# Two graph layers on one core: the first 24 index gathers read x in place of the projected source table

## The reference, cut to what matters

```python
def _L0_gnn_ref(h, edge_index, edge_feat, W1, b1, W2, b2, W3, b3, W4, b4):
    msg_input = concatenate([h[src], h[dst], edge_feat], axis=-1)
    messages = silu(msg_input @ W1 + b1) @ W2 + b2
    agg = segment_sum(messages, dst, num_segments=6250)
    h_new = silu(concatenate([h, agg], -1) @ W3 + b3) @ W4 + b4
    return h_new + h
def _L1_gnn_ref(h, edge_index, eps, W1, b1, W2, b2, gamma, beta):
    z = (1.0 + eps) * h + segment_sum(h[src], dst, num_segments=6250)
    r = relu(z @ W1 + b1) @ W2 + b2 + h
    return relu(layernorm(r) * gamma + beta)
x = layernorm(x + _L0_gnn_ref(x, ...))
x = layernorm(x + _L1_gnn_ref(x, ...))
```

## Time and profile before

| | us |
|---|---|
| three runs | 1515.1, 1518.32, 1519.86 |
| median | 1518.32 |
| the profiled execution, its own time | 1517.0 |
| its span | 1514.8 |
| first gather from `src_term` starts | 39.46 |
| last gather from `src_term` starts | 1028.6 |

### The profile page before, as it was taken

The page is one execution under the profiler, slowest core; times in us unless marked ns, Lnnn a source line. Parts: engine busy times, 40 slices in busy tenths (PEclk is TensorE's granted clock), DMA queues, the critical chain, the costliest instruction groups (busy, mean ns, idle before and its releaser), DMA issues.

```text
span 1514.8 us, 31192 instructions
## 1 busy us (share of the span) xinstructions
PE 1273.0 (84%) x8093; PEld 1046.3 (69%) x8093; DVE 1011.0 (67%) x2306; ACT 641.7 (42%) x1257; POOL 1103.0 (73%) x1164
## 2 busy tenths in 40 slices
PE   6577777777787889888888898975999999999993
PEld 6355556665565667676766776754899999998882
DVE  5578886577764566666666565653666778888866
ACT  3735455455554555556555555652111111111111
POOL 1777777777777777777777777776777777777771
PEclk9889999999998999999999999997999999999995
DMA  5423333333335444455445544432887778778731
GB/s 196 119 81 95 87 90 95 93 95 89 92 94 100 129 135 126 125 135 133 126 126 135 131 129 124 132 78 84 260 255 232 220 224 244 229 221 239 218 93 47
DMA packets 189124, 214.15 MB, mean 141 GB/s; under 512 B 60426, under 2 KB 149517, under 8 KB 189011
## 3 DMA queue, kind: packets, MB, share of 16 engines
q1 hardware_dynamic: 138399, 131.62, 28.4%
q0 software_dynamic: 36352, 74.52, 20.7%
q10 hardware_dynamic: 14260, 6.68, 1.5%
HBM read 202.74 MB, written 9.85 MB: 140 GB/s over the span
## 4 chain that ended last, share of the span: by engine, by line
POOL 47%; PE 29%; issue 16%; DMA 4%; DVE 3%; SPq 1%; ACT 0%; DVEq 0%; ACTq 0%; POOLq 0%
POOL gath L869 47%; PE bank L1404 10%; PE bank L1380 8%; PE bank L1332 4%; DMA gath<-src_term,src_col 2%; PE bank L1210 1%; PE bank L1220 1%; PE bank L1206 1%; PE bank L1366 1%; DMA dst_rows<-in_dst 1%; PE bank L1411 1%; PE bank L1353 1%; PE bank L1426 1%; SPq L655 0%; DVE st L1982 0%
## 5 line engine op out<-in xcount | busy, mean ns | idle before, releaser
L869 POOL DMA_INDIRECT gath<-src_term,src_col x784 | 751.4, 958 | 244.2 <-issue 236.0
L869 POOL DMA_INDIRECT gath<-layer_input,src_col x336 | 327.8, 975 | 105.9 <-issue 100.3
L1210 PE MATMUL bank<-gath,ident 128*128 128x512 f32 x392 | 224.2, 655 | 170.0 <-DMA gath<-src_term,src_col 169.7
L1206 PEld LDWEIGHTS bank<-terms_r,terms_l 128*128 128x128 f32 x1568 | 202.4, 195 | 52.6 <-issue 52.4
L1885 DVE TENSOR_SCALAR_CACHE_REDUCE terms_l<-dst_bc,node_col 64x512 f32<-64x512 int32 x196 | 221.2, 1129 | 15.7 <-issue 9.8
L1896 DVE TENSOR_TENSOR S<-S,bank 128x128 f32 x98 | 28.1, 287 | 292.0 <-PE bank L1222 176.0
L1220 PEld LDWEIGHTS bank<-oh,msg 128*128 128x128 f32 x1568 | 201.2, 204 | 29.1 <-issue 28.4
L1206 PE MATMUL bank<-terms_r,terms_l 128*128 128x128 f32 x1568 | 211.2, 279 | 3.3 <-ACT msg L1014 2.5
L1220 PE MATMUL bank<-oh,msg 128*128 128x128 f32 x1568 | 204.2, 287 | 0.0
L1210 PEld LDWEIGHTS bank<-gath,ident 128*128 128x128 f32 x392 | 61.2, 197 | 190.8 <-DMA gath<-src_term,src_col 190.7
L1404 PE MATMUL bank<-S 128*128 128x288 f32 x672 | 170.0, 406 | 0.9 <-DVE S L1955 0.9
(11 more groups left out here) (208 smaller groups left out, 1703.2 us busy)
## 6 DMA issues: line engine op xcount, KB each, us to landing
dst_bc<-in_dst SPq DMA_DIRECT2D x195, 128.0 KB
xT<-sorted_src SPq DMA_DIRECT2D x42, 512.0 KB
xs<-layer_input SPq DMA_DIRECT2D x136, 128.0 KB
gath<-src_term,src_col POOLq DMA_INDIRECT x784
terms_l<-layer_input SPq DMA_DIRECT2D x88, 128.0 KB
terms_r<-layer_input SPq DMA_DIRECT2D x88, 128.0 KB
msg<-layer_input SPq DMA_DIRECT2D x80, 128.0 KB
ef_s<-in_edge_attr SPq DMA_DIRECT2D x97, 64.0 KB
```

The costliest lines, as they stand in the source:

```text
L869: g.indirect_dma_start(out=gath[:, slot, j * D:(j + 1) * D], out_offset=None, in_=table[0:rows, :], in_offset=bass.IndirectOffsetOnAxis(ap ...
L1206: mm(bank[h][:, j * D:(j + 1) * D], terms_l[:, u, h, j, :], terms_r[:, u, h, j, :], start=j == 0, stop=False)
L1210: mm(bank[h][:, :], ident[:, :], gath[:, slot, :], start=False, stop=True).then_inc(pre_ps, 1)
```

## The change

Pairs 0 to 2 (`FROM_X = 3`, 24 gathers) read rows of the input x, into `xs`, `xTs` and `As`, and don't need the table. POOL waits for the table ahead of pair 3. PE turns the gathered rows at the steps 1 to 3, DVE copies them to the slots of `gath`, and PE multiplies them by the source weights and adds b1, in place of the one matmul by `ident`. The source indices are loaded behind block 1 of x and prepared in the steps 1 and 2 of the prologue; the destination parts move one or two steps back. POOL makes `terms_r` without waiting for `diag_made`.

```diff
+FROM_X = 3
@@ views
+        from_x = [xs[:, h, :, :].rearrange("p t d -> p (t d)") for h in range(2)] + [xTs[:, h, :] for h in range(2)] + \
+            [As[:, h, :, :].rearrange("p t d -> p (t d)") for h in range(2)]
@@ sync
-                    if b == 5:
+                    if b == 1:
                         load_rows(sp, src_rows, src, src_in)
                     elif b == 8:
                         load_rows(sp, dst_rows, dst, dst_in)
@@ gpsimd
-            pool.wait_ge(diag_made, 1)
@@ gather_sources
+                if k == FROM_X:
+                    source_table_stored()
                 for g in (2 * k, 2 * k + 1):
+                    if k < FROM_X:
+                        gather_rows(x, N, g, src_col[:, g * CH:(g + 1) * CH], gathered[g], from_x[g])
+                        continue
                     if g >= RING:
                         pool.wait_ge(pre_ps, done(g - RING))
...
-            source_table_stored()
             pool.wait_ge(src_ready, 1)
@@ tensor, prologue
-                6: lambda: turn_rows(src_rows_f, src_prep, None, src_turned), 9: spread_bases})))
+                1: lambda: turn_rows(src_rows_f, src_prep, None, src_turned), 10: spread_bases})))
@@ tensor, new
+            def turn_from_x(k):
+                for h in range(2):
+                    g = 2 * k + h
+                    pe.wait_ge(gathered[g], 16 * CH)
+                    for j in range(CH):
+                        last = nc.tensor.transpose(bank[5 + h][:, j * P:(j + 1) * P],
+                                                   from_x[g][:, j * D:(j + 1) * D], ident[:, :])
+                    last.then_inc(from_x_turned, 1)
+            def add_from_x(g, ps):
+                pe.wait_ge(from_x_kept, g + 1)
+                for j in range(CH):
+                    mm(ps[:, j * D:(j + 1) * D], gath[:, g, j * P:(j + 1) * P], wab[:, 0:D], start=False, stop=False)
+                for j in range(CH):
+                    last = mm(ps[:, j * D:(j + 1) * D], ident[:, :], b1_bc[:, :], start=False, stop=j == CH - 1)
+                last.then_inc(pre_ps, 1)
@@ pre_sums
+                    if isinstance(k, int) and k < FROM_X:
+                        add_from_x(g, bank[h])
+                        continue
@@ tensor, steps
-                  at_steps({4: weight_products}),
+                  at_steps({4: weight_products, **{k + 1: lambda k=k: turn_from_x(k) for k in range(FROM_X)}}),
@@ vector, prologue
-                4: lambda: to_float(src_rows, src_rows_f, src_in, src_prep),
-                5: lambda: to_float(dst_rows, dst_rows_f, dst_in, dst_prep), 6: least_dst, 7: diagonals,
-                8: lambda: cols_of(src_turned, src_col, P).then_inc(src_ready, 1), 10: window_bases})))
+                1: lambda: to_float(src_rows, src_rows_f, src_in, src_prep),
+                2: lambda: cols_of(src_turned, src_col, P).then_inc(src_ready, 1),
+                7: lambda: to_float(dst_rows, dst_rows_f, dst_in, dst_prep), 8: least_dst, 9: diagonals,
+                11: window_bases})))
@@ vector, new: first stage of the steps 2 to 4
+            def keep_from_x(k):
+                for h in range(2):
+                    g = 2 * k + h
+                    dve.wait_ge(from_x_turned, g + 1)
+                    ve_.tensor_copy(gath[:, g, :], bank[5 + h][:, :]).then_inc(from_x_kept, 1)
```

More of the change, by code:

```diff
@@ L309, in build @@
         one_eps_made = sem("one_eps_made")
+        from_x_turned = sem("from_x_turned")
+        from_x_kept = sem("from_x_kept")
         w2_turned = sem("w2_turned")
@@ L865, in _, with gather_rows @@
                                     ALU.mult).then_inc(wef_ready, 1)
-            def gather_rows(table, rows, slot, indices, gathered):
+            def gather_rows(table, rows, slot, indices, gathered, to=None):
+                to = gath[:, slot, :] if to is None else to
                 for j in range(CH):
                     g.indirect_dma_start(
-                        out=gath[:, slot, j * D:(j + 1) * D], out_offset=None, in_=table[0:rows, :],
+                        out=to[:, j * D:(j + 1) * D], out_offset=None, in_=table[0:rows, :],
                         in_offset=bass.IndirectOffsetOnAxis(ap=indices[:, j:j + 1], axis=0)).then_inc(gathered, 16)
@@ L2128, in any_order @@
                 all_units1(dve, rows1, norm1, norm2)
-            steps(dve, NPAIR - 2, range(1, SORTED + 2), at_steps({5: weight_products}), *in_banks(9, rows0),
+            steps(dve, NPAIR - 2, range(1, SORTED + 2), at_steps({
+                5: weight_products, **{k + 2: lambda k=k: keep_from_x(k) for k in range(FROM_X)}}), *in_banks(9, rows0),
                   of_early(4, add_early), of_pair(1, windows), of_pair(2, one_hots(0, sums_ps, oh_made)),
```

## The result

| | before | after |
|---|---|---|
| median of 4 runs each, us | 1519.09 | 1505.05 |
| lowest and highest, us | 1515.10, 1519.88 | 1503.47, 1505.89 |
| ratio | | 0.9905, 95% interval 0.9893 to 0.9917 |
| profiled execution, its own time / span, us | 1517.0 / 1514.8 | 1505.45 / 1503.6 |
| first gather of the kernel, us | 39.46 | 22.58 |

Faster by 14.0 us in the medians and by 11.55 between the two profiled executions. They compare fast runs alone: single runs of e1 (1972.43 us) and e12 (1646.35 us, at a mean granted clock of 0.739 in place of 0.951 to 0.955) were slow and are left out of them.

The account below looks back on a forecast made before the run. POOL's unbroken gather stream was taken to bound the first layer, its start moving its end: 1517.0 - 19.9 (earlier start) + 1.0 (gathers beside DVE) = 1498.1, forecast 1498 us, range 1493 to 1506.

Parts of the forecast that it names:

- first gather: Prologue: POOL's stream starts at 19.6 us instead of 39.5; 21.3 if the source rows land at 14, not 12.35.
- The signs: Start at 19 to 21, last gather from the table at 1009 to 1011, second layer at most 2 us longer.
- The sum: Whole kernel: 1517.0 of the profiled execution, less 19.9 at the start, plus 1.0 for gathers beside DVE, gives 1498.1 us.
- first 24 gathers: Pairs 0 to 2 on POOL: 31.2 us as before, plus 1.0 for running beside a busy DVE.
- The two casts: Prologue, DVE: casts of the source rows take 0.8 us, plus 0.5 for one collision with `terms_r`.
- PE's part: Prologue: PE turns the source rows in 1.07 us, then does the next block's turn, 0.60, and terms, 1.06.
- DVE's part: Prologue: DVE adds b1 (0.69) and orders xT (0.68), overlapping by some 0.1, then writes `src_col` in 1.1 us.
- The cover of the table: Ahead of pair 3: the table, stored at 38.66, is needed only at 50.8, so 12 us are to spare.
- rival 2: Prologue: DVE's copies and POOL's gathers block each other, up to 0.75 us a gather: 1515, half held 1506; chance 0.06.
- rival 1: First layer: slots of `gath` are late at group 14, POOL loses 8.6 us, about 1507; chance 0.13.
- Rivals 3 and 4: Table becomes the wait again, 1506 at 20 us delay, 0.04; stream earlier but end unchanged, within 0.3%, 0.03.
- Rival 5: Second layer: a lower granted TensorE clock lengthens PE's stretches, 1534 at a mean of 0.91; chance 0.03.

Follow-up runs that it names:

- e1: The kernel before, unchanged, run again on a slower chip: 1950.99 us, ratio 0.9984.
- e12: The changed kernel with `terms_r` made between the gathers of pair 0 and pair 1: 1496.21 us, ratio 0.9854 to before.
- e9: The changed kernel with `FROM_X = 0`, no gathers from x, on an ordinary chip: 1517.61 us, ratio 1.0001 to before.
- e6: The changed kernel with the load of 67 index rows split into 64 and 3, source and destination: 1497.81 us, ratio 0.9877 to before.
- e5: The changed kernel with POOL making `terms_r` only after both casts of the source rows: 1499.84 us, ratio 0.9891 to before.
- e10: The changed kernel with `FROM_X = 1`, 8 gathers from x, on an ordinary chip: 1506.45 us, ratio 0.9928 to before.
- e8: The changed kernel with source indices loaded and prepared ahead of x, loads split 64 and 3, `terms_r` between pairs 0 and 1: 1481.93 us, ratio 0.9770 to before.
- e7: The changed kernel with DVE writing `src_col` straight behind the casts, ahead of the next block: 1497.50 us, ratio 0.9875 to before.
- e3: The changed kernel with `FROM_X = 1`, 8 gathers from x, on the slower chip: 1938.72 us, ratio 0.9924 to before.
- e4: The changed kernel with `FROM_X = 2`, 16 gathers from x, on the slower chip: 1937.63 us, ratio 0.9911 to before.

## Why the prediction was right, and where its 7 us went

**The mechanism** was right in each step: the first layer is one stream of POOL, its start moved and its end with it, the table was early enough, and the slots were free. e9 shows that the earlier preparation is worth nothing without the gathers out of x.

**The signs** that the prediction gave came out less well than its range. The first gather (22.58) lies behind its 19 to 21, the last from the table (1014.7) behind its 1009 to 1011, and the second layer took 2.6 us longer, where more than 2 was to count against it. By the other profiles this last sign was set too narrow, as told below. The median is inside the range by only 1 us.

**The sum** was made between executions, 1517.0 to 1498.1, and the execution took 1505.45. The 7.35 us lie as follows:

| term | forecast | found | cost |
|---|---|---|---|
| first gather | 19.6 | 22.58 | +3.0 |
| first 24 gathers | 31.2 + 1.0 | 32.3 | +0.1 |
| 759 pitches up to the 784th | as before | 1.2646 for 1.2621 | +1.9 |
| end of the first layer to the second | as before | 26.0 for 25.97 | 0.0 |
| second layer | as before | 462.9 for 460.3 | +2.6 |
| outside the span | 2.2 | 1.85 | -0.35 |

- **The step that failed is the first gather.** "DVE asks behind its first block ... 12.35" was the end taken of a range whose other end, 14, was in the text: the source rows landed 11.08 us after their last issue, DVE waited 1.97, and the casts began at 14.11 (+1.8). The reason, shown by e6, is the DMA of 67 rows in one piece; the earlier trace rows showed the same for the destination rows, as SP's hold of 5.07 and the 9.56 to the landing, and both were read as a full queue. The 21.3 that the prediction gives for this case is 1.3 short, by PE's part below.
- **The two casts** took 1.63 us with the collision instead of 0.8 + 0.5: +0.3. The sort of collision was right (e5), its size a little more.
- **PE's part**, the turn of the rows and the block behind it, took 4.15 us (15.80 to 19.95) instead of 2.73: +1.4. Its matmuls took 1.58, 0.85 and 1.72 where the same ones take 1.07, 0.60 and 1.06 in the earlier trace rows. PE had stood idle for 5.04 us before. The trace of the kernel before shows such a price as well: eight L1152 took 2.07 at 8.87 after 3.23 us idle and 2.05 at 26.18 after 3.97, against 1.06. The prediction took all its PE terms from places where PE had not paused for long.
- **DVE's part** was 2.3 (20.0 to 22.29) as forecast, and POOL followed by 0.29 rather than 0.80: -0.5.
- **The cover of the table** was put at 12 us and was 14, by ACT's clearing of `S`. e10 shows the wait that one pair less than two brings: 6.8.
- **The gathers beside DVE**, rival 2: 1.0 was right. There are single ones of 1.51 and 1.61; the median of the first pair is 1.054, and that of the second and third 0.958. DVE copies and adds blocks of x all the while. Its copy `xT<-gath` at 24.01 (0.70) begins with the second gather, and that gather takes 1.51, 0.55 more than usual. But the copy at 22.82 (0.66) lies wholly within the first gather, which takes 1.15 there and 1.12 in e8 with DVE idle beside it. So a copy can hold a gather up for most of its own length, and need not hold it up at all.
- **The slots**, rival 1: 1.5 us to spare were forecast, 11 were found. Group 6 was used at 84.3, not at 89.8, and POOL came for its slot at 95.25, not at 91.3. A part of that is a slip in the sum: it takes off 0.56 for each L1210, but the earlier trace rows has some 1.12 for one (two records). With it PE's added work is 3.2 us a pair and 9.6 in all, not 12.9, group 6 would be used at 86.5, 4.8 us were to spare, and rival 1 would have cost 5.3 at its worst, not 8.6. The other 6 are the later start of POOL's stream (some 4) and 2 us of PE that no term had. PE's waits for gathers fell from 169.7 to 120.5 in all. e8, which starts 14 us earlier still, doesn't stall there either.
- **Rivals 3 and 4** didn't happen: no wait for the table, and of the 16.9 us by which the stream starts earlier, 13.9 are there at the 784th gather. **Rival 5** didn't either: PE's clock in the second layer is granted 1.00 as before.
- **The pitch and the second layer** took 4.5 us that no term had: the sum took both as before. The added work of PE and DVE is not the reason, since e7, e6 and e5 have all of it and a pitch of 1.2599 to 1.2617. The second layer took 459.4 to 462.0 in the eight profiles of the experiments on ordinary chips; before's 460.3 and the 462.9 of after are two draws of that, with this one just above it. e9, the nearest thing to a second profile of before on an ordinary chip, has 1.2608 and 460.7. The 0.958 of the gathers looks like this execution's or this chip's too: its second-layer gathers take 0.947, where before and all eight others have 0.944, and e7, whose program for POOL is the same, has 0.955. A second profile of the changed kernel was not taken, so this stays an argument.

So of the 7 us, 3 were a mis-sized start. The rest is most likely the spread between executions, which a sum from one trace can't see.

## What to carry to other kernels

Where one engine issues an unbroken stream, look for what its first instruction waits for, and give it work that needs less of the prologue: here 16 gathers out of the raw input cover the building of the table, and a third pair brings nothing more. Then look at what stands between the raw indices and the first instruction: an awkwardly sized load, a block of other work in the order of an in-order engine, or a neighbour's operation can each hold the start by 1 to 4 us. The load and the block came out at the end clear of the intervals, the neighbour's 0.84 us is too small to be told there. Spare of the slots should be worked out with the waits that disappear, since extra work of an engine that waits is paid out of those waits first.

## What the runs showed of the hardware

- **The order of POOL's program changes how long a gather takes.** 0.944 us in e8 and e12, 0.955 to 0.958 in the others, for the same instruction with the same data; with its idle time the pitch is 1.250 to 1.251 against 1.260 to 1.265, some 8 us over the first layer. Both chips on which 0.944 was seen have 0.955 with the other kernels. In both fast kernels `terms_r` stands between pair 0 and pair 1, which changes the program of POOL. The 16 gathers of the bridge change in the same way (0.944 against 0.955 to 0.958), while the second layer's take 0.944 to 0.947 in all of them, before among them. What in it does this, the place of the code or something else, wasn't isolated.
- **67 rows in one DMA are slower than 64 and 3, and hold back others.** The source rows landed 11.08 us after the last issue, the one-row load behind the destinations' 67 rows held SP for 5.68 us, and W1 landed 6.5 us after its issue. With the split (e6) DVE no longer waited for the rows, the hold was 0.25 and W1 took 4.0.
- **Casts and copies beside POOL's tensor_tensor** are held up: 1.25 to 1.27 instead of 0.42 for the second cast of the change and both of e6 and e7, 4.71 instead of 0.7 for a copy in e8. The first cast of the change, at 0.45, wasn't. Of the first pair's eight gathers beside DVE four take the usual 0.96, the others 1.15 to 1.51.
- **PE after a pause.** Eight records of matmuls took 1.58 us after 5.04 us idle, and 1.07 in the prologue of the kernel before, while the granted clock in that stretch reads 1.00:

```profile
15.80:20.00 4.20, 4.20 (x22) 4.20 (x23) 0.03 (x1) 0.59 (x1) 0.84 (x1) 1.00 0.58 202
```

The next block's eight, at 20.27, took 1.06 again. What makes the first ones longer is not shown by any run here.
- **Chips differ.** The kernel before takes 1517 to 1519 us on the chips of most runs, and 1952 on one, with a mean granted clock of 0.86 against 0.955 and the waits of POOL shown with e1. With one and two pairs from x the gain there was 13 to 14 us as well (e3, e4).
